# First self attention: the output projection by three products of split factors

## The chip, the core and the metric

One core of a Trainium2 chip runs the whole program. Its engines work side by side, each through its own queue in order, and meet at semaphores: TensorE (PE, matmuls, with its weight loads shown as PEld), VectorE (DVE), ScalarE (ACT), GpSimd (POOL) and SyncE (SP, which issues most DMAs). The metric is the device time of one execution in microseconds (us), the median of several runs.

## What is computed

Two transformer layers on x of shape 4 x 1024 x 256, f32. The change lies in the first step, the self attention of layer 0, followed by a residual and a layer norm:

```python
xq = jnp.einsum('bsh,oh->bso', x, wq)      # likewise xk, xv; 1024 outputs
xq = xq.reshape(bsz, N_HEADS, seqlen, HEAD_DIM)   # here 4 x 16 x 1024 x 64
scores = jnp.einsum('bhid,bhjd->bhij', xq, xk) * SCALE
scores = jax.nn.softmax(scores, axis=-1)
out = jnp.einsum('bhij,bhjd->bhid', scores, xv)
out = out.reshape(bsz, seqlen, N_HEADS * HEAD_DIM)
return jnp.einsum('bso,ho->bsh', out, wo)         # the output projection
...
x = _layernorm(x + _L0_attn_ref(x, ...), axis=-1)
```

The reshape makes a head of 64 token rows: 64 heads, each with 1024 x 1024 scores. The other steps (cross attention, a mixture of experts, a second self attention, a second cross attention, an MLP on chosen tokens) are not touched.

## The kernel before

`layer0_self_attention` works through 16 groups of 256 token rows, four heads each (j = 0 to 3); groups 1 to 13 are a hardware loop over `group`. Each engine walks the same Python code and emits only its own instructions, so the order of the code is the order of every queue, and `w.inc` / `w.at` keep the semaphore counts.

**A head** has four steps p = 0 to 3. In each, PE computes two of the eight 128-row blocks of transposed scores (`scores`, L726 to L732, into `psS`), ACT takes two exponentials of 128 x 1024 (`exponent`, L745, into the ring `pr`), POOL adds them to `total` (`add_up`, L760, seven adds per head), and PE multiplies the step before by V (`values`, L774, into `psO`). Meanwhile PE, DVE and ACT find the row maxima of the next head (`largest` L618/L619 and L626, `on_diagonal` L635, which I call `diag`), and after p = 3 `spread` (L645) brings them into `psX`, from where `seed_new` (L680 on DVE, L685 on ACT) and `keep_least` (L654, L658) set up `psS` for the next head.

**A head's end.** `take_out` (L784, ACT) copies `psO` to `oU`, without the softmax's division. The sum of the head's exponentials comes during the next head: at p = 1 PE sums `total` (`misc` "S", L441), DVE transposes and inverts (`turn_back`, L486, L793, L794, at p = 2), and POOL multiplies `oU` by the inverse (`divide`, L804, at p = 2, behind the adds of that step) into `oT`, two heads side by side. `take_out` of the next head waits for `ot`, so that `oU` is free:

```python
        def take_out(w):
...
                w.wait("pv", w.at("pv"))
                w.wait("ot", w.at("ot"))
                w.eng.activation(oU[:, :], psO[:, :], ACT.Copy).then_inc(sems["nm"], 1)
```

**Side tasks** (`misc`) fill PE between the steps; `TASKS` lists them by head and place. The Q and K projections of the next group (L427, six fp32r products of split factors) stand at p = 1, at p = 2 and twice at a head's end ("e"), where the first goes into `psM` and the second into `psO`: the second waits until `take_out` has read `psO`. The output projections ("O", L447, f32, eight products of 128 x 128 by 128 x 256 each, which the trace shows as sixteen matmuls) stand at p = 0 of heads 1 and 3. The residual, moments (`moments`), `root` (four small operations on POOL, L522 to L525, at p = 2) and `norm_out` (L534 on ACT, at p = 3) of the projected 128 rows follow in the same head; heads 0 and 2 have none of these.

**At the start**, `split` divides a weight matrix into a high part in fp32r (ACT) and the rest (DVE, L897 and L900), for wq, wk and wv. `wo` is used as it is.

Of the kernel before, what the change touches and what calls it, by code (L numbers as in the profile page):

```python
# [12 lines left out]
P = 128  # L13
D = 256
# [290 lines left out]
def layer0_self_attention(nc, x, wqT, wkT, wvT, woT, y):  # L305
# [13 lines left out]
    with ExitStack() as ctx:  # L319
        m = Room(nc, ctx, "a")  # L320
        wqh, wql, wkh, wkl, wvh, wvl = (m.sb(n, [P, 2, SEG * HD], F32R) for n in ("wqh", "wql", "wkh", "wkl", "wvh", "wvl"))
        wo = m.sb("wo", [P, KC, D])
# [31 lines left out]
        oT = m.sb("oT", [P, 2, KC, P])  # L354
# [14 lines left out]
                 "ad", "pv", "nm", "rec", "ot", "var", "pl", "rstd", "y", "yo", "dv")  # L369
# [36 lines left out]
        def misc(w, what, G, buf, k="M", more=True, out=True):  # L406
# [4 lines left out]
            if w.on("tensor"):  # L411
# [17 lines left out]
                elif kind == "V":  # L429
                    _, tt, c2 = what  # L430
                    if not out:
                        w.wait("wl", 3)
                    w.wait("xl", w.at("xl"))
                    for n, (xp, wp) in enumerate(((xh, wvh), (xh, wvl), (xl, wvh))):
                        for cc in range(2):
                            last = w.eng.matmul(ps[:, :], xp[:, cc, tt * P:(tt + 1) * P], wp[:, cc, c2 * 512:(c2 + 1) * 512],
                                                start=n == 0 and cc == 0, stop=n == 2 and cc == 1)
                elif kind == "S":
                    w.wait("ad", w.at("ad", 3 if more else 0))
                    for q in range(2):  # L440
                        last = w.eng.matmul(ps[q * HD:(q + 1) * HD, :], ones[:, 0:HD].bitcast(F32), total[:, buf, q * 512:(q + 1) * 512],  # L441
                                            start=True, stop=True)
                elif kind == "O":
                    w.wait("w", 16)
                    w.wait("ot", w.at("ot"))
                    for c in range(KC):
                        last = w.eng.matmul(ps[:, 0:D], oT[:, buf, c, :], wo[:, c, :], start=c == 0, stop=c == KC - 1)  # L447
# [29 lines left out]
            elif kind == "V":  # L477
                _, tt, c2 = what
                if w.on("scalar"):
                    w.wait("bv", w.at("bv"))  # L480
                    w.wait("mi", w.at("mi"))
                    w.eng.activation(vg[:, tt, c2 * 512:(c2 + 1) * 512], ps[:, :], ACT.Copy).then_inc(sems["ma"], 1)
# [316 lines left out]
        def divide(w, j):  # L799

            if w.on("gpsimd"):
                w.wait("nm", w.at("nm"))
                w.wait("rec", w.at("rec"))
                w.eng.tensor_tensor(oT[:, j // 2, :, (j % 2) * HD:(j % 2 + 1) * HD],  # L804
                                    oU[:, :].rearrange("p (c t) -> p c t", t=HD),
                                    rec[:, :].rearrange("p (c t) -> p c t", t=HD), ALU.mult).then_inc(sems["ot"], 1)
            w.inc("ot")

        def group(w, G, first=False, left=2):
# [17 lines left out]
            for j in range(GH):  # L827
# [11 lines left out]
                for p in range(KC // 2):  # L839
# [3 lines left out]
                    for i in (2 * p, 2 * p + 1):  # L843
                        exponent(w, i)
                        add_up(w, i, j % 2)
# [21 lines left out]
                    if p == 2 and not start:  # L867
                        turn_back(w)
                        divide(w, (j - 1) % GH)
# [20 lines left out]
        def walk(w):  # L890
            w.came = {}
            turns = ["S0", "S1", "S2", "S3", "0", "1", "M"]
            def split(n):
                hi, lo, full = ((wqh, wql, pr[:, 0:2, :]), (wkh, wkl, pr[:, 2:4, :]), (wvh, wvl, total[:, :, :]))[n]
                if w.on("scalar"):
                    w.wait(("wq", "wk", "wv")[n], 16)
                    w.eng.activation(hi[:, :, :], full, ACT.Copy).then_inc(sems["wh"], 1)  # L897
# [8 lines left out]
            for i in range(2 * KC):  # L906
                if i in (3, KC):
                    split((3, KC).index(i) + 1)
# [32 lines left out]
            divide(w, GH - 1)  # L941
# [26 lines left out]
        def _(eng):  # L968
            for t, src, n in ((pr[:, 0:2, :], wqT, "wq"), (pr[:, 2:4, :], wkT, "wk"), (total[:, :, :], wvT, "wv")):
                eng.dma_start(t, src.rearrange("(a p) o -> p a o", p=P)).then_inc(sems[n], 16)  # L970
            eng.dma_start(wo[:, :, :], woT.rearrange("(c p) e -> p c e", p=P)).then_inc(sems["w"], 16)
# [2032 lines left out]
```

## Time and profile before

| what | value |
|---|---|
| median of 3 runs | 2907.83 us (2907.33 to 2910.18) |
| profiled execution | 2896.75 us, its span 2895.0 us |
| PE busy | 2533.0 us, 87% |
| POOL, DVE, ACT busy | 56%, 63%, 54% |
| mean granted clock of PE | 0.937 of full speed |

The first self attention takes the first 1690 us of the span. A share of the span averages over stages with different limits; the stretch of a stage, and the timeline of one head in it, tell what ends a wait. A row of the timeline gives the start, the duration and, in brackets, how long the engine was idle before it and whose work ended that.

### The profile page before, as it was taken

Reading aid. Unit: us, or ns where it says so; the run is one execution under the profiler, and the core shown is the slowest. Engines: PE = TensorE matmul, PEld = TensorE weight load, DVE = VectorE, ACT = ScalarE, POOL = GpSimd, SP = SyncE. Lnnn points to the kernel's source line nnn. Section 1 sums busy time; section 2 is a strip of 40 time slices with the busy share of each in tenths; the row PEclk is TensorE's granted clock in tenths of the full one; section 3 lists DMA queues with packets and bytes.
Section 4 is the critical chain, followed back from the end, with each engine's and each line's share of the span. In section 5 each row is a group of like instructions: output and inputs, shape, how many; then the busy total and the mean of one; then the engine's idle time right before and its main releaser. Section 6 shows DMA issues by size and latency. Waiting matters only on the chain. (4 is left out here: it accounts for less than half of the span.)

```text
span 2895.0 us, 43888 instructions
## 1 busy us (share of the span) xinstructions
PE 2533.0 (87%) x12067; PEld 1413.7 (49%) x12067; DVE 1822.8 (63%) x3044; ACT 1576.4 (54%) x2568; POOL 1621.6 (56%) x1344
## 2 busy tenths in 40 slices
PE   6999999999999999999999959971994688698595
PEld 4554555555555555555554434540673344454264
DVE  4776777777777777777777635662334565468743
ACT  4666676766667676666766625640222343454334
POOL 2777677777767777776777733424334213333343
PEclk8999999999999999999999979985997699899798
DMA  7454444555445455545544220003992100000242
GB/s 185 121 132 117 124 129 123 136 126 130 121 123 129 122 136 127 130 121 124 129 122 107 57 93 2 2 20 124 382 341 92 32 0 1 31 2 10 57 127 88
DMA packets 413442, 309.49 MB, mean 107 GB/s; under 512 B 296951, under 2 KB 341407, under 8 KB 408351
## 3 DMA queue, kind: packets, MB, share of 16 engines
q1 hardware_dynamic: 397118, 238.27, 31.8%
q0 software_dynamic: 12272, 63.92, 6.3%
q10 hardware_dynamic: 3952, 6.08, 0.6%
q8 instruction: 50, 0.82, 0.1%
q14 instruction: 50, 0.40, 0.1%
HBM read 193.33 MB, written 94.13 MB: 99 GB/s over the span
## 5 line engine op out<-in xcount | busy, mean ns | idle before, releaser
L760 POOL TENSOR_TENSOR a_total<-a_total,a_pr 128x1024 f32<-128x1024 f32 x384 | 915.5, 2384 | 268.9 <-ACT a_pr L745 251.1
L626 DVE TENSOR_REDUCE a_nmax<-a_psX 128x1 f32<-128x1024 f32 x512 | 623.8, 1218 | 279.8 <-PE a_psX L619 279.8
L745 ACT ACTIVATE a_pr<-a_psS 128x1024 f32<-128x1024 f32 x512 | 496.5, 1022 | 364.1 <-PE a_psS L732 344.1
L774 PE MATMUL a_psO<-a_pr,a_vd 128*64 128x512 f32 x2048 | 492.5, 602 | 0.0
L726 PE MATMUL a_psS<-a_qA,a_kA 128*128 128x512 f32 x1024 | 292.1, 406 | 8.3 <-DVE a_psS L680 4.4
L618 PE MATMUL a_psX<-a_kA,a_qA 64*128 64x512 f32 x512 | 232.8, 455 | 35.5 <-DVE a_nmax L626 31.3
L760 POOL TENSOR_TENSOR a_total<-a_pr 128x1024 f32<-128x1024 f32 x64 | 152.1, 2377 | 192.5 <-ACT a_pr L745 192.5
L774 PEld LDWEIGHTS a_psO<-a_pr,a_vd 128*64 128x64 f32 x2048 | 129.9, 136 | 241.6 <-issue 240.5
L696 DVE COPY a_psS<-a_least 128x1024 f32<-128x1024 f32 x192 | 232.6, 1212 | 4.6 <-ACT a_pr L745 4.6
L635 ACT ACTIVATE a_diag<-a_ident,a_nmax 128x128 fp32r<-128x128 f32 x512 | 186.0, 401 | 88.1 <-DVE a_nmax L626 88.1
L619 PE MATMUL a_psX<-a_kB,a_qA 64*128 64x512 f32 x512 | 232.8, 455 | 0.0
L618 PEld LDWEIGHTS a_psX<-a_kA,a_qA 64*128 64x128 f32 x512 | 94.7, 185 | 238.1 <-DVE a_nmax L626 146.2
L726 PEld LDWEIGHTS a_psS<-a_qA,a_kA 128*128 128x128 f32 x1024 | 173.2, 190 | 58.4 <-issue 21.2
L705 ACT ACTIVATE a_psS<-a_least 128x1024 f32<-128x1024 f32 x192 | 197.0, 1026 | 0.3
L732 PE MATMUL a_psS<-a_qB,a_kB 64*128 64x512 f32 x512 | 187.6, 446 | 0.0
L730 PE MATMUL a_psS<-a_qB,a_kA 64*128 64x512 f32 x512 | 187.6, 446 | 0.0
L1204 DVE TENSOR_REDUCE c_nmx<-c_psM 128x4 f32<-128x308 f32 x256 | 109.6, 468 | 50.4 <-PE c_psM L1199 49.5
L680 DVE COPY a_psS<-a_psX 128x512 f32<-128x512 f32 x126 | 81.7, 694 | 82.9 <-PE a_psX L645 82.9
L447 PE MATMUL a_psM<-a_wo,a_oT 128*128 128x256 f32 x512 | 121.5, 391 | 3.3 <-POOL a_oT L804 3.3
L730 PEld LDWEIGHTS a_psS<-a_qB,a_kA 64*128 64x128 f32 x512 | 75.8, 185 | 93.6 <-issue 93.6
L2692 ACT ACTIVATE e_hT<-e_psH,e_wt 128x128 f32<-128x128 f32 x156 | 44.6, 368 | 127.9 <-PE e_psH L2684 127.9
L447 PEld LDWEIGHTS a_psM<-a_wo,a_oT 128*128 128x128 f32 x512 | 96.4, 193 | 27.0 <-issue 14.7
(423 smaller groups left out, 4881.1 us busy)
## 6 DMA issues: line engine op xcount, KB each, us to landing
a_qA<-a_qhi SPq DMA_DIRECT2D x248, 128.0 KB, 2.7
a_qB<-a_qlo SPq DMA_DIRECT2D x124, 256.0 KB, 3.8
a_vd<-a_vg SPq DMA_DIRECT2D x128, 128.0 KB, 2.3
a_kA<-a_khi SPq DMA_DIRECT2D x124, 128.0 KB, 2.6
a_kA<-a_klo SPq DMA_DIRECT2D x62, 256.0 KB, 3.6
a_qhi<-a_ph SPq DMA_DIRECT2D x120, 128.0 KB, 2.0
a_qlo<-a_pl SPq DMA_DIRECT2D x120, 128.0 KB, 2.1
a_khi<-a_ph SPq DMA_DIRECT2D x120, 128.0 KB, 2.0
```

What stands on the lines that cost most here:

```text
L447: last = w.eng.matmul(ps[:, 0:D], oT[:, buf, c, :], wo[:, c, :], start=c == 0, stop=c == KC - 1)
L618: w.eng.matmul(psX[:, 0, :], qA[0:HD, b, u * P:(u + 1) * P], kA[0:HD, b, 0:512], start=True, stop=True)
L619: w.eng.matmul(psX[:, 1, :], qA[HD:P, b, u * P:(u + 1) * P], kB[HD:P, b, :], start=True, stop=True)\
L626: w.eng.tensor_reduce(nmax[:, u:u + 1], psX[:, :, :].rearrange("p a k -> p (a k)"), AX.X, ALU.max, negate=True)\
L696: w.eng.tensor_copy(both(psS[:, 0, :, :]), least[:, :]).then_inc(sems["sv"], 1)
L705: w.eng.activation(both(psS[:, 1, :, :]), least[:, :], ACT.Copy).then_inc(sems["sa"], 1)
L726: w.eng.matmul(psS[:, n, q, :], kA[:, b, kc * P:(kc + 1) * P], qA[:, b, q * 512:(q + 1) * 512], start=False, stop=False, skip_group_check= ...
L730: low = w.eng.matmul(psS[:, 0, q, :], kA[0:HD, b, p * P:(p + 1) * P], qB[0:HD, b, cols], start=False, stop=True, skip_group_check=True)
L732: high = w.eng.matmul(psS[:, 1, q, :], kB[HD:P, b, p * P:(p + 1) * P], qB[HD:P, b, cols], start=False, stop=True, skip_group_check=True)
L745: w.eng.activation(pr[:, n, :], both(psS[:, i % 2, :, :]), ACT.Exp, scale=SCALE).then_inc(sems["e"], 1)
L760: w.eng.tensor_tensor(total[:, buf, :], first, pr[:, n, :], ALU.add).then_inc(sems["ad"], 1)
L774: last = w.eng.matmul(psO[q * HD:(q + 1) * HD, :], vd[:, b, kc, :], pr[:, n, q * 512:(q + 1) * 512], start=p == 0 and i == 0, stop=p == KC ...
```

## The change

Both factors of the output projection are split into a high part rounded to fp32r and the rest, and the projection becomes three fp32r products, high x high, high x low and low x high: 24 matmuls of 256 columns in place of eight f32 products. For that

- `divide` multiplies `oU` in place and signals `dq`, no longer `ot`;
- a new `split_out` copies `oU` to `oh` on ACT, after the eighth exponential of the head (i = 7), and subtracts on POOL, `oU - oh` into `ol`, between the adds of i = 6 and i = 7; this subtraction now signals `ot`, on which `take_out`, the projection, `turn_back` and the first add of a head wait as before;
- `woT` is loaded into `vg` at the start and split into `woh` and `wol` ahead of the thirteenth of sixteen Q and K pieces (i = 12), and the first write of `vg` by the V projections waits for that.

```diff
         wqh, wql, wkh, wkl, wvh, wvl = (m.sb(n, [P, 2, SEG * HD], F32R) for n in ("wqh", "wql", "wkh", "wkl", "wvh", "wvl"))
-        wo = m.sb("wo", [P, KC, D])
+        woh, wol = (m.sb(n, [P, KC, D], F32R) for n in ("woh", "wol"))
         ident = m.sb("ident", [P, P])
...
         inv = m.sb("inv", [P, 512 // 32])
-        oT = m.sb("oT", [P, 2, KC, P])
+        oh, ol = (m.sb(n, [P, 2, KC, P], F32R) for n in ("oh", "ol"))
         res = m.sb("res", [P, 2, D])
...
-                 "ad", "pv", "nm", "rec", "ot", "var", "pl", "rstd", "y", "yo", "dv")
+                 "ad", "pv", "nm", "rec", "dq", "oh", "ot", "var", "pl", "rstd", "y", "yo", "dv")
         sems = {n: m.sem(n) for n in names + tuple(f"so{n}" for n in range(PIECES))}
...
                 elif kind == "O":
-                    w.wait("w", 16)
+                    w.wait("wl", 4)
                     w.wait("ot", w.at("ot"))
-                    for c in range(KC):
-                        last = w.eng.matmul(ps[:, 0:D], oT[:, buf, c, :], wo[:, c, :], start=c == 0, stop=c == KC - 1)
+                    for n, (op, wp) in enumerate(((oh, woh), (oh, wol), (ol, woh))):
+                        for c in range(KC):
+                            last = w.eng.matmul(ps[:, 0:D], op[:, buf, c, :], wp[:, c, :],
+                                                start=n == 0 and c == 0, stop=n == 2 and c == KC - 1)
                 last.then_inc(sems["mi"], 1)
...
                     w.wait("bv", w.at("bv"))
+                    if not out:
+                        w.wait("wl", 4)
                     w.wait("mi", w.at("mi"))
...
-        def divide(w, j):
+        def divide(w):
             if w.on("gpsimd"):
                 w.wait("nm", w.at("nm"))
                 w.wait("rec", w.at("rec"))
-                w.eng.tensor_tensor(oT[:, j // 2, :, (j % 2) * HD:(j % 2 + 1) * HD],
-                                    oU[:, :].rearrange("p (c t) -> p c t", t=HD),
-                                    rec[:, :].rearrange("p (c t) -> p c t", t=HD), ALU.mult).then_inc(sems["ot"], 1)
+                w.eng.tensor_tensor(oU[:, :], oU[:, :], rec[:, :], ALU.mult).then_inc(sems["dq"], 1)
+            w.inc("dq")
+
+        def split_out(w, j):
+
+
+            def chunks(t):
+                return t[:, j // 2, :, (j % 2) * HD:(j % 2 + 1) * HD]
+
+            whole = oU[:, :].rearrange("p (c t) -> p c t", t=HD)
+            if w.on("scalar"):
+                w.wait("dq", w.at("dq"))
+                w.eng.activation(chunks(oh), whole, ACT.Copy).then_inc(sems["oh"], 1)
+            w.inc("oh")
+            if w.on("gpsimd"):
+                w.wait("dq", w.at("dq"))
+                w.wait("oh", w.at("oh"))
+                w.eng.tensor_tensor(chunks(ol), whole, chunks(oh).bitcast(F32), ALU.subtract).then_inc(sems["ot"], 1)
             w.inc("ot")
...
                         exponent(w, i)
+                        if i == KC - 1 and not start:
+                            split_out(w, (j - 1) % GH)
                         add_up(w, i, j % 2)
...
                         turn_back(w)
-                        divide(w, (j - 1) % GH)
+                        divide(w)
                     if p == 3 and outs:
...
             def split(n):
-                hi, lo, full = ((wqh, wql, pr[:, 0:2, :]), (wkh, wkl, pr[:, 2:4, :]), (wvh, wvl, total[:, :, :]))[n]
+                hi, lo, full = ((wqh, wql, pr[:, 0:2, :]), (wkh, wkl, pr[:, 2:4, :]), (wvh, wvl, total[:, :, :]),
+                                (woh, wol, vg[:, :, :].rearrange("p a (c e) -> p (a c) e", e=D)))[n]
                 if w.on("scalar"):
-                    w.wait(("wq", "wk", "wv")[n], 16)
+                    w.wait(("wq", "wk", "wv", "w")[n], 16)
                     w.eng.activation(hi[:, :, :], full, ACT.Copy).then_inc(sems["wh"], 1)
...
             for i in range(2 * KC):
-                if i in (3, KC):
-                    split((3, KC).index(i) + 1)
+                if i in (3, KC, KC + 4):
+                    split((3, KC, KC + 4).index(i) + 1)
                 misc(w, ("QK"[i // KC], i % KC), 0, 0, turns[i % 7], out=False)
...
             turn_back(w)
-            divide(w, GH - 1)
+            divide(w)
+            split_out(w, GH - 1)
             misc(w, ("O",), NG - 1, 1)
...
                 eng.dma_start(t, src.rearrange("(a p) o -> p a o", p=P)).then_inc(sems[n], 16)
-            eng.dma_start(wo[:, :, :], woT.rearrange("(c p) e -> p c e", p=P)).then_inc(sems["w"], 16)
+            eng.dma_start(vg[:, :, :].rearrange("p a (c e) -> p (a c) e", e=D), woT.rearrange("(c p) e -> p c e", p=P))\
+                .then_inc(sems["w"], 16)
             eng.preload_act_table(ACT.Exp)
             eng.wait_ge(sems["cst"], 5)
             walk(Writer(nc, eng, "scalar", sems))
```

POOL's order at the end of an odd head (head 3 of the first group, from p = 0): `a_total` is the running sum, `a_rstd` the four operations of `root`. Before:

```order
L760 TENSOR_TENSOR a_total<-a_total,a_pr 128x1024 x4
L522 TENSOR_TENSOR a_rstd<-a_mv,a_eps 128x1
L523 TENSOR_TENSOR a_rstd<-a_rstd,a_mhalf 128x1
L524 TENSOR_TENSOR a_rstd<-a_mv,a_rstd 128x1
L525 TENSOR_TENSOR a_rstd<-a_zero,a_rstd 128x1
L804 TENSOR_TENSOR a_oT<-a_oU,a_rec 128x8x64
L760 TENSOR_TENSOR a_total<-a_total,a_pr 128x1024 x2
```

After:

```order
L764 TENSOR_TENSOR a_total<-a_total,a_pr 128x1024 x4
L526 TENSOR_TENSOR a_rstd<-a_mv,a_eps 128x1
L527 TENSOR_TENSOR a_rstd<-a_rstd,a_mhalf 128x1
L528 TENSOR_TENSOR a_rstd<-a_mv,a_rstd 128x1
L529 TENSOR_TENSOR a_rstd<-a_zero,a_rstd 128x1
L808 TENSOR_TENSOR a_oU<-a_oU,a_rec 128x512
L764 TENSOR_TENSOR a_total<-a_total,a_pr 128x1024
L825 TENSOR_TENSOR a_ol<-a_oU,a_oh 128x8x64
L764 TENSOR_TENSOR a_total<-a_total,a_pr 128x1024
```

One 128 x 512 operation, the subtraction, has come between the last two adds, and the signal that frees `oU` has moved behind it.

ACT's order at the same head's end, from the step p = 3 on: `a_pr` are the last two exponentials, `a_diag` `on_diagonal`, `a_res` `norm_out`, `a_oU` `take_out`, the two `a_psS` `seed_new`, `a_least` `keep_least`. Before, behind the exponentials:

```order
L745 ACTIVATE a_pr<-a_psS 128x1024 x2
L635 ACTIVATE a_diag<-a_ident,a_nmax 128x128 x2
L534 ACTIVATE a_res<-a_res,a_rstd 128x256
L635 ACTIVATE a_diag<-a_ident,a_nmax 128x128
L784 ACTIVATE a_oU<-a_psO 128x512
L685 ACTIVATE a_psS<-a_psX 128x512 x2
L658 ACTIVATE a_least<-a_psX 128x512
```

After, with the exponentials:

```order
L749 ACTIVATE a_pr<-a_psS 128x1024 x2
L820 ACTIVATE a_oh<-a_oU 128x8x64
L639 ACTIVATE a_diag<-a_ident,a_nmax 128x128 x2
L538 ACTIVATE a_res<-a_res,a_rstd 128x256
L639 ACTIVATE a_diag<-a_ident,a_nmax 128x128
L788 ACTIVATE a_oU<-a_psO 128x512
L689 ACTIVATE a_psS<-a_psX 128x512 x2
L662 ACTIVATE a_least<-a_psX 128x512
```

The copy stands ahead of everything with which ACT ends the head.

## Rows read from the trace of the kernel before

**Rows 1.** The page, part 1: busy us, share of the span, instructions.

```profile
PE 2533.0 (87%) x12067; PEld 1413.7 (49%) x12067; DVE 1822.8 (63%) x3044; ACT 1576.4 (54%) x2568; POOL 1621.6 (56%) x1344
```

**Rows 2.** Windows: us, each engine's busy us, granted clock, DMA share, GB/s.

```profile
700.00:1000.00 300.00, 296.19 (x1483) 159.21 (x1483) 217.60 (x276) 205.61 (x345) 220.23 (x120) 1.00 0.50 127
```

**Rows 3.** Timeline, PE: start us, us, line, out<-in, count [idle, releaser].

```profile
787.96 0.51 PE L427 MATMUL a_psM<-a_xh,a_wkh 128*128 128x256 f32 x2
...
788.78 1.09 PE L726 MATMUL a_psS<-a_qA,a_kA 128*128 128x512 f32 x4
...
798.78 3.72 PE L447 MATMUL a_psM<-a_wo,a_oT 128*128 128x256 f32 x16
802.43 0.50 PE L618 MATMUL a_psX<-a_kA,a_qA 64*128 64x512 f32 x1
```

**Rows 4.** Timeline, POOL, an even head's end.

```profile
737.11 4.84 POOL L760 TENSOR_TENSOR a_total<-a_total,a_pr 128x1024 f32<-128x1024 f32 x2 [2.59 <-ACT a_pr L745]
741.91 1.28 POOL L804 TENSOR_TENSOR a_oT<-a_oU,a_rec 128x512 f32<-128x512 f32 x1
743.14 4.84 POOL L760 TENSOR_TENSOR a_total<-a_total,a_pr 128x1024 f32<-128x1024 f32 x2
```

**Rows 5.** Timeline, ACT, the same head's end.

```profile
741.05 1.94 ACT L745 ACTIVATE a_pr<-a_psS 128x1024 f32<-128x1024 f32 x2 [1.37 <-PE a_psS L732]
742.88 0.69 ACT L635 ACTIVATE a_diag<-a_ident,a_nmax 128x128 fp32r<-128x128 f32 x2
744.69 0.40 ACT L635 ACTIVATE a_diag<-a_ident,a_nmax 128x128 fp32r<-128x128 f32 x1 [1.12 <-DVE a_nmax L626]
745.31 0.60 ACT L784 ACTIVATE a_oU<-a_psO 128x512 f32<-128x512 f32 x1 [0.21 <-PE a_psO L774]
745.96 1.07 ACT L685 ACTIVATE a_psS<-a_psX 128x512 f32<-128x512 f32 x2
```

**Rows 6.** Timeline, PE, the same head's end.

```profile
745.19 0.73 PE L645 MATMUL a_psX<-a_diag,a_ones 128*128 128x512 f32 x2
...
746.47 0.40 PE L427 MATMUL a_psO<-a_xh,a_wqh 128*128 128x256 f32 x2
...
747.19 1.09 PE L726 MATMUL a_psS<-a_qA,a_kA 128*128 128x512 f32 x4
```

**Rows 7.** Timeline, POOL, an odd head's end.

```profile
716.82 1.27 POOL L804 TENSOR_TENSOR a_oT<-a_oU,a_rec 128x512 f32<-128x512 f32 x1
718.04 4.87 POOL L760 TENSOR_TENSOR a_total<-a_total,a_pr 128x1024 f32<-128x1024 f32 x2
```

**Rows 8.** Timeline, ACT, the same odd head's end.

```profile
716.96 0.59 ACT L534 ACTIVATE a_res<-a_res,a_rstd 128x256 f32<-128x256 f32 x1
718.27 0.40 ACT L635 ACTIVATE a_diag<-a_ident,a_nmax 128x128 fp32r<-128x128 f32 x1 [0.72 <-DVE a_nmax L626]
718.88 0.60 ACT L784 ACTIVATE a_oU<-a_psO 128x512 f32<-128x512 f32 x1 [0.21 <-PE a_psO L774]
```

**Rows 9.** Timeline, PE, the same odd head's end.

```profile
718.76 0.73 PE L645 MATMUL a_psX<-a_diag,a_ones 128*128 128x512 f32 x2
...
720.04 0.40 PE L427 MATMUL a_psO<-a_xh,a_wkh 128*128 128x256 f32 x2
```

**Rows 10.** Timeline, ACT, the last head.

```profile
1669.86 0.60 ACT L784 ACTIVATE a_oU<-a_psO 128x512 f32<-128x512 f32 x1 [0.68 <-POOL a_oT L804]
```

**Rows 11.** Timeline, DVE, at the start.

```profile
24.15 2.29 DVE L900 TENSOR_TENSOR a_wvl<-a_total,a_wvh 128x2048 fp32r<-128x2048 f32 x1 [0.49 <-ACT a_wvh L897]
```

**Rows 12.** Timeline, PE, and one window: two idles close together.

```profile
1581.73 0.49 PE L618 MATMUL a_psX<-a_kA,a_qA 64*128 64x512 f32 x1 [1.32 <-DVE a_nmax L626]
...
1582.86 2.07 PE L726 MATMUL a_psS<-a_qA,a_kA 128*128 128x512 f32 x4 [0.64 <-DVE a_psS L696]
...
1631.01 1.27 PE L726 MATMUL a_psS<-a_qA,a_kA 128*128 128x512 f32 x4 [0.63 <-DVE a_psS L696]
...
1583.00:1587.00 4.00, 4.00 (x14) 2.19 (x16) 1.55 (x2) 1.23 (x2) 1.58 (x1) 0.62 0.37 103
```

## The prediction

> **What bounds the kernel now.** I read the page first. TensorE (PE) is busy for 87% of the span, ahead of VectorE (DVE, 63%) and GpSimd (POOL, 56%) [rows 1]. The average hides that the changed stage is tighter: from 700 to 1000 us, in the middle of the first self attention, PE is busy for 296.19 of 300 us at a granted clock of 1.00, while ScalarE (ACT) has 205.61 and POOL 220.23 [rows 2]. PE sets the pace there, so a microsecond taken from PE is a microsecond of time, and a microsecond for which PE is made to wait is one too. There is 1% of slack to absorb it. ACT and POOL have a third and a quarter of their time free on average, but the change asks for them at one place, the end of each head, so I then read the timeline there engine by engine. There are two kinds of head end: 64 heads, of which those with j = 0 or 2 (even) have a plain end, and those with j = 1 or 3 (odd) carry the layer norm of a finished block too.
>
> **The output projection.** Before, one f32 projection is 8 products that the trace shows as 16 matmuls of 256 columns. It starts at 798.78 and the next matmul at 802.43: 3.65 us, 0.228 each [rows 3]. After, it is 24 fp32r products of 256 columns with other weights each time, the same form as the Q and K pieces. A piece of six behind `largest` takes from 787.96 to 788.78, 0.82 us [rows 3]; a piece in the middle of a stream 746.47 to 747.19, 0.72 us, 0.12 each [rows 6]. So 24 take 0.82 + 18 x 0.12 = 2.98 us, and a projection gets 0.67 us cheaper. There are 32 of them; 31 lie in the PE-bound stretch: **-20.8 us**. The matmuls rise by half in number and still cost less, since each takes half the time. The Trainium skill (TensorE: Matmul & The Clock Gate, Back-to-back issue gap) gives an isolated gap of columns / 2.4 GHz plus 2.5 ns, 109 ns for 256 columns; by that, a projection would be an estimated 2.6 us and the sum some 11 us lower. The row says 120 ns, so I keep the row.
>
> **What is added at a head's end.** The division now writes `oU` in place (same size, 1.28 us, no change). Behind the head's last exponential ACT copies `oU` to `oh` (128x512; the like copy L784 takes 0.60 us), and POOL subtracts `oU - oh` into `ol` (like L804, 1.28 us) between the last two adds. The word that decides is in a line that the diff doesn't touch: `take_out`, which copies the next head's `psO` over `oU`, waits for `ot`. Before, `ot` came with the division. Now it comes with the subtraction, because `oU` is still read by it. `take_out` stands in ACT's queue ahead of the two seed copies, the copy to `least` and the next head's exponentials, and PE waits for it before the second projection piece, which writes `psO`.
>
> **Even head's end, step by step.** POOL is busy without a break from 737.11: two adds, the division to 743.19, two adds to 747.98 [rows 4]. The sixth index's add ends at 743.14 + 2.38 = 745.52, so the subtraction can't start before 745.5, and ends at 745.47 + 1.28 = 746.75 (a start without a dependency comes 0.05 us before the end of the one ahead, as the division's does). ACT's own new copy is hidden: the exponentials end at 742.99 [rows 5], the division at 743.19, so the copy runs from 743.3 to 743.9 and two `diag` (0.69) to 744.6, before the third `diag` at 744.69, for which ACT waited 1.12 us. `take_out` started at 745.31, as soon as PE's last value product let it [rows 5]. It now waits for POOL to 746.75 + 0.10 = 746.85 (the 0.10 is the step from `diag`'s end, 745.09, to `spread` at 745.19 [rows 5, 6]), and ends at 747.45. PE's piece into `psO` began at 746.47 [rows 6]; now 747.55. With 0.11 for a first matmul after a wait, PE loses **1.19 us**. The seeds, 0.65 us behind `take_out`, are then just in time: the first ends at 748.1, when the scores begin at 748.4.
>
> **Odd head's end.** Four small layer-norm operations go ahead of the division, which therefore ends at 718.09, and the first add behind it at 718.04 + 2.39 = 720.43 [rows 7]. The subtraction: 720.38 to 721.66. ACT is hit earlier as well: its copy waits for the division, 718.19 to 718.79, and behind it queue two `diag`, the norm's 0.59 and the third `diag`, which ended at 718.67 and now ends near 720.4 [rows 8]. `spread` on PE slips from 718.76 to 720.5 [rows 9], a stall of 1.7 us that is a part of the whole, not more: `take_out` starts at 721.76, not 718.88 [rows 8], ends at 722.36, and the `psO` piece starts at 722.46, not 720.04 [rows 9]. With the 0.11: **2.53 us**.
>
> **Count.** The first split is issued in head 1, which has no norm yet. Short stalls: head 1 and the even heads 2 to 62, 32 x 1.19 = 38.1. Long stalls: odd heads 3 to 61, 30 x 2.53 = 75.9. In heads 58 to 62 there is no projection piece, but the next scores wait for ACT's seeds, behind the same `take_out`. Together **+114.0 us**. Nothing gives this back: each head's first exponential depends on the scores, and POOL, which then has its pause of 2.59 us before the fourth index [rows 4], is free in time. That a wait on this edge costs ACT real time is seen once before, in the last head, where `take_out` waited 0.68 us for L804 [rows 10].
>
> **Start and end.** The start gets a split of `woT` (a copy on ACT and, like the other weights' one, 2.29 us on DVE) ahead of the thirteenth of sixteen projection pieces. DVE works there without a pause, and the later pieces wait: **+2.3 us** [rows 11]; below, it could be nothing, above twice that, if ACT's copy counts as well. At the end the last add comes 1.28 later, copy and subtraction add 0.10 + 0.60 + 0.10 + 1.28 = 2.08 before the last projection, and that one saves about 1: **+2.4 us**.
>
> **Clock.** In this stage the clock stays at 1.00. The rows show what idling does: PE idled 1.32 us before 1581.73 and 0.64 before 1582.86; then four score matmuls took 2.07 us, and from 1583 to 1587 the granted clock was 0.62, a mix of 2.4 and 1.2 GHz: 0.38 x 4 = 1.5 us lost. Behind the like pair 48 us later, whose second idle is 0.63, the same matmuls took 1.27 us: nothing lost [rows 12]. An odd head's end now has two idles, 1.6 and 0.7 us, further apart than that pair; an even one has a single idle of 1.1, shorter than the first of that pair. I allow for a drop in one odd head of five: 30 x 0.2 x 1.5 = **+9 us**.
>
> **Sum.** -20.8 + 114.0 + 2.3 + 2.4 + 9 = +107 us. The profiled execution took 2896.75 us (span 2895.0) and would become 3004; the median of the runs, 2907.83, lies 11 us above it, so I forecast 3015 us, a ratio of 1.037.
>
> **Rivals.**
> (1) The clock drops in every odd head: 45 us in place of 9, 3051 us. For it: two idles with 2.3 us of waiting. Against: the pair above is denser and fell once and stayed once. The Trainium skill (TensorE: Matmul & The Clock Gate, Part 1) says that the gate goes by how busy PE was of late and knows two rates; by that this rival's chance hangs on how close together the two idles lie.
> (2) The other side: the copy and the subtraction are hidden as they look by the averages, because `take_out` doesn't come behind the subtraction. This decides at the point where the subtraction ends: before 745.3 in an even and 718.8 in an odd head it would cost nothing, and the rest would be -20.8 + 4.7 = -16 us, 2892 us. For it: POOL is idle for a quarter. Against: POOL has no gap between 737.11 and the head's end, and misses those points by 1.5 and 2.9 us, with every operation in that count taken from a row.
> (3) A part is absorbed: the stalls are there, but seeds, reductions and adds that were late catch up in them, so that half of the price stays: 2955 us. For it: 1.3% of PE's time in the stage is idle, waits that a shift could swallow [rows 2]. Against: that is 1.3 us per group of four heads, which come behind the scores and move along with them.
> (4) The fp32r projections cost what an f32 matmul costs, 0.228 each: 5.5 us in place of 3.65, 31 x 1.8 = 56 us in place of -20.8: 3092 us. Against: rows 6.
>
> **How the numbers follow.** Forecast 0.80; (1) 0.09; (2) 0.04; (3) 0.05; (4) 0.02. Unknown sizes: stalls of 1.08 and 2.42 without the first-matmul term (-7), a projection cheaper by 0.8 (-4), no clock loss (-9), start -2: about 2992. Upwards the clock in every odd head: 3051. Range 2990 to 3052. About 0.2% is what a measurement of this kernel can tell from no change; faster by more than that 0.04 (rival 2), within it 0.01, slower 0.95.
>
> **What would show it.** In the profile after: ACT's `take_out` group with idle time before it, ended by POOL's `ol`, about 1.8 us in 32 heads and, behind a later `diag`, 1.4 in 30, near 100 us in all; `oh` waits for POOL, little in even heads and over a microsecond in odd ones; a group of four heads takes 6 us more (2 x 1.19 + 2 x 2.53 - 2 x 0.67); PE's busy share from 700 to 1000 falls from 99% to about 92%; a projection takes 3.0 us. The forecast is wrong if `take_out` doesn't wait, or if PE's waits before `psO` are well below 1 us.

## The result, and the profile after

| | before | after |
|---|---|---|
| median, six runs each, side by side | 2906.68 us (2902.31 to 2910.18) | 3005.76 us (3003.2 to 3009.68) |
| profiled execution | 2896.75 us | 3004.84 us |

The kernel became slower by a ratio of 1.0343 (95% interval 1.033 to 1.0357): 99 us between the medians, 108 between the two profiled executions. The forecast was 3015 us, +107.

The page's first part and the window of [rows 2], after:

```profile
PE 2544.6 (85%) x12323; PEld 1425.4 (47%) x12323; DVE 1827.9 (61%) x3045; ACT 1609.6 (54%) x2633; POOL 1698.0 (57%) x1408
...
700.00:1000.00 300.00, 278.85 (x1430) 150.63 (x1429) 203.82 (x255) 199.33 (x337) 219.50 (x124) 0.99 0.47 119
```

PE's busy time from 700 to 1000 us fell from 296.19 to 278.85 us, from 99% to 93%. No other engine took its place as the bound: ACT and POOL are both at or below where they were in [rows 2]. PE waits. For whom, the view of the waits says (0 to 1800 us; engine, tile and line that waits, whose work ended the wait, us in total, how often, the longest):

```profile
ACT a_oU L788 <- POOL a_ol L825: 107.1, 63, 2.5
...
ACT a_oh L820 <- POOL a_oU L808: 69.5, 64, 7.0
...
PE a_psO L427 <- ACT a_oU L788: 47.1, 57, 0.9
PE a_psX L649 <- ACT a_diag L639: 40.1, 30, 1.4
```

The chain can be read off: the subtraction (L825, POOL) holds up `take_out` (L788, ACT) in 63 heads, `take_out` holds up the piece into `psO` (PE) 57 times by 0.83 us on the mean, and in 30 odd heads a late third `diag` (L639) holds up `spread` (L649) by 1.34 us.

**An even head's end**, the timeline (start, us, line, out<-in, count, idle before and who ended it) of POOL, ACT and PE, answering [rows 4 to 6]:

```profile
779.59 2.38 POOL L764 TENSOR_TENSOR a_total<-a_total,a_pr 128x1024 f32<-128x1024 f32 x1
781.92 1.28 POOL L808 TENSOR_TENSOR a_oU<-a_oU,a_rec 128x512 f32<-128x512 f32 x1
783.15 2.38 POOL L764 TENSOR_TENSOR a_total<-a_total,a_pr 128x1024 f32<-128x1024 f32 x1
785.46 1.31 POOL L825 TENSOR_TENSOR a_ol<-a_oU,a_oh 128x512 fp32r<-128x512 f32 x1
786.70 2.41 POOL L764 TENSOR_TENSOR a_total<-a_total,a_pr 128x1024 f32<-128x1024 f32 x1
...
783.24 0.63 ACT L820 ACTIVATE a_oh<-a_oU 128x512 fp32r<-128x512 f32 x1 [0.33 <-POOL a_oU L808]
783.77 0.68 ACT L639 ACTIVATE a_diag<-a_ident,a_nmax 128x128 fp32r<-128x128 f32 x2
784.69 0.40 ACT L639 ACTIVATE a_diag<-a_ident,a_nmax 128x128 fp32r<-128x128 f32 x1 [0.24 <-DVE a_nmax L630]
786.87 0.60 ACT L788 ACTIVATE a_oU<-a_psO 128x512 f32<-128x512 f32 x1 [1.77 <-POOL a_ol L825]
...
787.52 0.51 PE L427 MATMUL a_psO<-a_xh,a_wqh 128*128 128x256 f32 x2 [0.89 <-ACT a_oU L788]
```

POOL has no gap in this stretch, with the subtraction behind the first of the two adds. ACT's new copy is done at 783.87, long before it is needed: not the copy, but POOL's queue sets the subtraction's start. The subtraction ends at 786.77 and `take_out` starts 0.10 later. The third `diag` is on time, and PE loses its time once, ahead of `psO`.

**An odd head's end**, the same views, answering [rows 7 to 9]:

```profile
752.95 1.27 POOL L808 TENSOR_TENSOR a_oU<-a_oU,a_rec 128x512 f32<-128x512 f32 x1
754.18 2.35 POOL L764 TENSOR_TENSOR a_total<-a_total,a_pr 128x1024 f32<-128x1024 f32 x1
756.49 1.29 POOL L825 TENSOR_TENSOR a_ol<-a_oU,a_oh 128x512 fp32r<-128x512 f32 x1
...
754.25 0.63 ACT L820 ACTIVATE a_oh<-a_oU 128x512 fp32r<-128x512 f32 x1 [1.67 <-POOL a_oU L808]
...
755.87 0.39 ACT L639 ACTIVATE a_diag<-a_ident,a_nmax 128x128 fp32r<-128x128 f32 x1
757.87 0.60 ACT L788 ACTIVATE a_oU<-a_psO 128x512 f32<-128x512 f32 x1 [1.62 <-POOL a_ol L825]
...
756.30 0.72 PE L649 MATMUL a_psX<-a_diag,a_ones 128*128 128x512 f32 x2 [1.36 <-ACT a_diag L639]
...
758.52 0.80 PE L427 MATMUL a_psO<-a_xh,a_wkh 128*128 128x256 f32 x2 [0.79 <-ACT a_oU L788]
```

Here the division comes later, so the copy waits for it, and the `diag` behind it in ACT's queue has no idle time before it any more (0.72 in [rows 8]): it runs as soon as the queue lets it. PE idles twice, 1.36 and 0.79 us. In this head the clock fell as well: the piece took 0.80 where [rows 9] have 0.40, and from 758 to 762 the granted clock was 0.57.

**The projection**, PE's timeline, answering [rows 3]:

```profile
790.26 1.21 PE L448 MATMUL a_psM<-a_woh,a_oh 128*128 128x256 f32 x8
791.31 1.10 PE L448 MATMUL a_psM<-a_wol,a_oh 128*128 128x256 f32 x8
792.24 1.10 PE L448 MATMUL a_psM<-a_woh,a_ol 128*128 128x256 f32 x8
793.27 0.50 PE L622 MATMUL a_psX<-a_kA,a_qA 64*128 64x512 f32 x1
```

24 products from 790.26 to 793.27, 3.01 us, against 3.65.

**Where the 108 us are.** I measured each head as the time from the end of its predecessor's last exponential to the end of its own, in both traces. What follows an even head got longer by 0.50 us behind head 0 of a group and by 0.43 behind head 2 (medians of the heads without a drop of the clock), which is a stall of about 1.1 less the 0.6 or so that a projection gained; what follows an odd head got longer by 2.41 to 2.44, and by 3.7 to 3.9 where the clock fell. Head 1, the first with a stall, has no norm yet; what follows it got longer by 1.05. Up to the last head's last exponential that comes to 1.05 + 31 x 0.465 + 30 x 2.43 + 1.5 at the start = 89.9 us. The measured shift there is 101.9 us, and the 12 left over go with the clock: ten stretches at half clock (1.2 of 2.4 GHz) up to that point (at 168, 543, 758, 1188, 1403 and 1618 us, and behind heads 58 to 61, where no projection pieces are left), against one before. Behind the last head the stage's end costs another 1.9. The last 4 us lie in the later stages, whose code is the same and whose length differs by more than that between the profiled executions of this case (1206 to 1218 us).

### The profile page after: what moved, and what is told of

Read it like the earlier page. It is cut to its first block and busy times, and to the rows that moved or that the text cites. A ratio compares the mean times of both kernels' runs of the same rounds, so it can differ in the third digit from the quotient of the medians.

```text
span 3003.0 us, 44611 instructions
## 1 busy us (share of the span) xinstructions
PE 2544.6 (85%) x12323; PEld 1425.4 (47%) x12323; DVE 1827.9 (61%) x3045; ACT 1609.6 (54%) x2633; POOL 1698.0 (57%) x1408
## 5 line engine op out<-in xcount | busy, mean ns | idle before, releaser
L730 PE MATMUL a_psS<-a_qA,a_kA 128*128 128x512 f32 x1024 | 299.0, 413 | 10.9 <-DVE a_psS L684 4.4
L639 ACT ACTIVATE a_diag<-a_ident,a_nmax 128x128 fp32r<-128x128 f32 x512 | 184.7, 396 | 33.5 <-DVE a_nmax L630 33.5
L475 DVE TENSOR_TENSOR a_pl<-a_psM,a_ph 128x256 fp32r<-128x256 f32 x177 | 73.9, 417 | 80.2 <-ACT a_ph L471 78.4
L1212 POOL CAST c_qR<-c_qF 128x512 fp32r<-128x512 f32 x64 | 40.4, 633 | 114.9 <-ACT c_qF L1207 114.8
```

Of the source, the lines that this page charges most:

```text
L639: w.eng.activation(diag[:, u * P:(u + 1) * P], ident[:, :], ACT.Copy, scale=nmax[:, u:u + 1]).then_inc(sems["dg"], 1)
L730: w.eng.matmul(psS[:, n, q, :], kA[:, b, kc * P:(kc + 1) * P], qA[:, b, q * 512:(q + 1) * 512], start=False, stop=False, skip_group_check= ...
```

## The experiments

The forecast was near, so the question is whether it was near for its reasons. The theory: `take_out` comes one to one behind the subtraction; in odd heads the wait of ACT's copy for the division is nested inside that; the fp32r product itself is a gain; the clock adds some. The rivals: the two waits of an odd head add up; the product isn't cheaper; something else than the release of `oU` sets the price. "`take_out` at +3.96" means 3.96 us after the end of the head's last exponential. It stood at +2.4 to +2.5 before in nearly all heads, and stands at +3.96 in even heads and +5.27 in odd ones after (medians).

### The product back to f32

```diff
                 elif kind == "O":
...
-                    for n, (op, wp) in enumerate(((oh, woh), (oh, wol), (ol, woh))):
-                        for c in range(KC):
-                            last = w.eng.matmul(ps[:, 0:D], op[:, buf, c, :], wp[:, c, :],
-                                                start=n == 0 and c == 0, stop=n == 2 and c == KC - 1)
+                    for c in range(KC):
+                        last = w.eng.matmul(ps[:, 0:D], oh[:, buf, c, :], woh[:, c, :], start=c == 0, stop=c == KC - 1)
```

`oh` and `woh` become f32 copies. The subtraction, the copies and the split of the weights stay in place, but the low factors aren't used.

> Changed kernel with the projection back to one f32 product (the copy goes into an f32 tile, the subtraction and the split of the weights are still done, their results not used for the product). Everything else and all orders as in the changed kernel. Theory: a projection takes 3.65 us again in place of 2.98, so 31 x 0.67 = 21 us more than the changed kernel, 3026 us. If the fp32r products gained nothing: 3006. If they gained as by 109 ns a matmul: 3037.

Measured: 3030.26 us (3027.9 to 3040.83), ratio 1.044 (1.0422 to 1.0457). A projection, PE's timeline:

```profile
798.22 3.72 PE L449 MATMUL a_psM<-a_woh,a_oh 128*128 128x256 f32 x16
801.87 0.50 PE L622 MATMUL a_psX<-a_kA,a_qA 64*128 64x512 f32 x1
```

3.65 us again, and the heads with a projection are 0.64 us longer than in the changed kernel (median): 32 x 0.64 = 20 of the 25 us between the two medians. The profiled execution was the slowest of this kernel's, 10 us above its median. In it the heads together are 28 us longer than in the changed kernel, the 20 and the clock, whose half-clock time is worth 18 single stretches against 13. The stalls are the same. So the arithmetic is a gain of 0.64 us each time, and the loss lies in the split's waits and in what they cost of the clock. Rival (4) falls.

### The subtraction one add earlier

```diff
-                    for i in (2 * p, 2 * p + 1):
-                        exponent(w, i)
-                        if i == KC - 1 and not start:
-                            split_out(w, (j - 1) % GH)
-                        add_up(w, i, j % 2)
+                    if p == 3 and not start:
+                        exponent(w, 6)
+                        exponent(w, 7, early=1)
+                        split_out(w, (j - 1) % GH)
+                        add_up(w, 6, j % 2, 1)
+                        add_up(w, 7, j % 2)
...
```

Both last adds now come behind the subtraction in POOL's queue; `early` and the added argument only keep the counts of the semaphores right.

> Changed kernel with GpSimd's subtraction ahead of the add of i=6 instead of behind it; ScalarE's copy stays behind the last exponential. Theory (take_out waits for the subtraction): from the trace after, z being the end of a head's last exponential, the copy ends at z+1.0 in an even and z+2.3 in an odd head, the subtraction at z+2.4 and z+3.7, so take_out starts at z+2.5 in even heads (before the change 2.3 to 2.5, after it 3.95) and at z+4.0 in odd ones (5.27), there held by ScalarE's own queue, no longer by GpSimd. Stalls: 32 x 0.1 and 30 x 1.8 = 57 us in place of about 111, so about 2946 us. Rival A (the extra 1.9 us of work on two engines costs this, wherever it stands in the queues): as after, 3006 us. Rival B (only GpSimd's place in the queue matters, ScalarE's copy is hidden everywhere): 2890 us.

Measured: 2934.09 us (2925.8 to 2934.25), ratio 1.0101 (1.0083 to 1.012), some 70 us less than the changed kernel. Even heads lose nothing any more (`take_out` at +2.47); odd heads have it at +3.79 and lose 1.35 to 1.43 each. POOL at the end of an odd head, and the waits from 100 to 1690 us:

```profile
777.55 1.28 POOL L808 TENSOR_TENSOR a_oU<-a_oU,a_rec 128x512 f32<-128x512 f32 x1
779.63 1.27 POOL L825 TENSOR_TENSOR a_ol<-a_oU,a_oh 128x512 fp32r<-128x512 f32 x1 [0.81 <-ACT a_oh L820]
780.85 4.87 POOL L764 TENSOR_TENSOR a_total<-a_total,a_pr 128x1024 f32<-128x1024 f32 x2
...
ACT a_oU L788 <- POOL a_ol L825: 7.3, 26, 0.3
...
PE a_psX L649 <- ACT a_diag L639: 40.2, 30, 1.4
```

The wait for the subtraction fell from 107 us (0 to 1800 us; 99.6 in this window) to 7, although every instruction is still there. One add's place in a queue was worth some 70% of the loss. The wait for `diag` stayed, and the odd heads lose 1.4 us with it. I had expected 1.8 per odd head, and `take_out` at +4.0, held by ACT's own queue; it came at +3.79, and POOL still held it in 26 heads, by 0.3 us at most.

### Two buffers for `oU`

```diff
-        oU = m.sb("oU", [P, 512])
+        oU = m.sb("oU", [P, 2, 512])
...
-        def take_out(w):
+        def take_out(w, b, back):
...
-                w.wait("ot", w.at("ot"))
-                w.eng.activation(oU[:, :], psO[:, :], ACT.Copy).then_inc(sems["nm"], 1)
+                w.wait("ot", w.at("ot", back))
+                w.eng.activation(oU[:, b, :], psO[:, :], ACT.Copy).then_inc(sems["nm"], 1)
...
-                take_out(w)
+                take_out(w, b, 1)
```

`take_out` writes the other buffer and waits for the subtraction of the head before (`back` = 1). For room, the inverse sums are written over `turned`, with a wait for that. The order on all engines is that of the changed kernel.

> Changed kernel with two buffers oU in turn, so that take_out doesn't wait for the subtraction of the head before but for that of two heads before; rec is written over turned to make room; orders of all queues unchanged. Theory: take_out no longer waits for GpSimd in any head; even heads lose nothing, odd heads still lose 1.75 to 1.85 us, since ScalarE's copy waits for the division with the third diag, and so spread, queued behind it. 30 x 1.8 = 54 us of stalls, about 2944 us, the same as with the subtraction moved. Rival A (the extra work itself): 3006. Rival B (only take_out's wait counts): 2890.

Measured: 2935.71 us (2933.47 to 2936.12), ratio 1.0114 (1.0097 to 1.0131). The waits from 100 to 1690 us:

```profile
ACT a_oU L788 <- PE a_psO L778: 7.7, 32, 0.3
...
PE a_psX L649 <- ACT a_diag L639: 40.1, 30, 1.4
```

`take_out` never waits for POOL, with the subtraction where the changed kernel has it. Even heads lose 0, odd ones 1.4 (expected: 1.8): the same as in the last experiment, by the other way. So the price of an even head is the release of `oU` and nothing else, and an odd head has a second price of 1.4 behind it.

### ACT's copy behind the third `diag`

```diff
                 values(w, KC // 2 - 1, b)
                 if more:
                     on_diagonal(w, KC - 1)
+                if not start:
+                    split_out(w, (j - 1) % GH, "copy")
                 take_out(w)
```

One buffer again, and the subtraction at the changed kernel's place. Only the copy moves, to where nothing waits behind it but `take_out`.

> Changed kernel with one buffer and GpSimd's order as it is; only ScalarE's copy is moved from behind the last exponential to behind the third diag, so spread is no longer late in odd heads. Theory (in odd heads the two delays lie inside one another: take_out waits for the subtraction in any case): odd heads gain nothing, take_out stays at z+5.3 and the scores' delay at 2.45 us; PE idles once for 2.4 us instead of 1.3 and 0.8. Even heads lose 0.25 us more, since the copy now ends at z+2.7 and the subtraction starts 0.25 later. 3006 + 32 x 0.25 = 3014 us, plus 1.4 us for each clock drop that the longer single idle brings (up to 40). Rival (the two delays add up, 1.4 for spread and 1.1 for take_out): 3006 - 30 x 1.4 = 2964 us.

Measured: 3033.31 us (3027.92 to 3034.37), ratio 1.0446 (1.0429 to 1.0463), slower than the changed kernel (ratio 1.0343). An odd head's end on POOL and ACT, and PE behind it:

```profile
760.95 1.27 POOL L808 TENSOR_TENSOR a_oU<-a_oU,a_rec 128x512 f32<-128x512 f32 x1
762.18 2.39 POOL L764 TENSOR_TENSOR a_total<-a_total,a_pr 128x1024 f32<-128x1024 f32 x1
764.51 1.27 POOL L828 TENSOR_TENSOR a_ol<-a_oU,a_oh 128x512 fp32r<-128x512 f32 x1
...
762.40 0.40 ACT L639 ACTIVATE a_diag<-a_ident,a_nmax 128x128 fp32r<-128x128 f32 x1 [0.72 <-DVE a_nmax L630]
762.71 0.62 ACT L821 ACTIVATE a_oh<-a_oU 128x512 fp32r<-128x512 f32 x1
765.88 0.60 ACT L788 ACTIVATE a_oU<-a_psO 128x512 f32<-128x512 f32 x1 [2.55 <-POOL a_ol L828]
...
766.52 0.50 PE L427 MATMUL a_psO<-a_xh,a_wkh 128*128 128x256 f32 x2 [2.19 <-ACT a_oU L788]
```

The third `diag` is on time again, 0.72 idle before it as in [rows 8]. It gave nothing: `take_out` of odd heads still stands at +5.26 (median), and PE has its waits as one idle of 2.19 in place of 1.36 and 0.79. The two waits of an odd head are nested, as the prediction had it ("a part of the whole, not more"), and the rival in which they add up (2964 us) falls. In even heads the copy came a little too late now (+4.22, 32 x 0.26 = 8 us). The clock took most of the rest: up to the last head, half-clock time worth 24 single stretches against 13 in the changed kernel (two of whose ten are longer), which at 1.4 us each is 15 us. 8 + 15 = 23, and the heads together got longer by 24.5.

### Two buffers, the whole split at the head's very end

```diff
                         exponent(w, i)
-                        if i == KC - 1 and not start:
-                            split_out(w, (j - 1) % GH)
                         add_up(w, i, j % 2)
...
+                if not start:
+                    split_out(w, (j - 1) % GH)
```

This is on top of the two buffers, and the count for which `take_out` waits moves along. The added lines stand behind the Q and K pieces of the head's end. The edit is meant to free ACT's queue ahead of the third `diag`.

> As with two buffers, and copy and subtraction stand at the very end of a head's code, behind the projection pieces' copies and all seven adds, where ScalarE idles before the next head's first exponential (about 1 us) and GpSimd idles before its first add (1.7 to 3 us). Theory: no stall is left in any head; what stays is the projection's gain of 0.67 us x 31, 1.5 us at the start and about 2 at the end: 2889 to 2893 us, faster than the kernel before by 0.5%. Rival A (the extra work itself costs): near 3006. Rival C (the copy now delays the next head's first exponential by up to 0.6 us in every head): 2893 + 38 = 2930.

Measured: 2918.38 us (2915.24 to 2920.06), ratio 1.0056 (1.0039 to 1.0072). A miss: 2889 to 2893 was expected. PE at the projection, POOL's subtraction ahead of it, and the waits from 0 to 1800 us:

```profile
751.21 1.27 POOL L825 TENSOR_TENSOR a_ol<-a_oU,a_oh 128x512 fp32r<-128x512 f32 x1 [0.74 <-ACT a_oh L820]
...
752.63 1.20 PE L447 MATMUL a_psM<-a_woh,a_oh 128*128 128x256 f32 x8 [0.68 <-POOL a_ol L825]
...
PE a_psM L447 <- POOL a_ol L825: 31.0, 32, 5.4
```

All waits at the head's end are gone, and a new one took their place: the projection, at p = 0 of the next head, needs the subtraction that was just put off. The heads with a projection gain some 0.6 and lose 1.0. The others lose nothing, so the late copy itself costs nothing.

### Two buffers, the split placed by its reader

A projection reads the outputs of two heads, and stands at p = 0 of heads 1 and 3. The split issued in head 0 or 2 is the later one of its two and is read at once. The split issued in head 1 or 3 is read a whole head later. So it stays at p = 3 in heads 0 and 2, which have no layer norm that delays the division, and goes to the very end in heads 1 and 3. This is on top of the two buffers:

```diff
-                        if i == KC - 1 and not start:
+                        if i == KC - 1 and b == 0 and not start:
                             split_out(w, (j - 1) % GH)
...
-                take_out(w, b, 1)
+                take_out(w, b, 1 - b)
...
+                if b == 1:
+                    split_out(w, j - 1)
```

> Two buffers oU, and the place of the split by head: in heads 0 and 2 copy and subtraction stay at p = 3 (the two-buffer run lost nothing there), in heads 1 and 3 they stand at the head's very end (the late-split run lost nothing by that copy; its loss was the projection of the next head waiting for a subtraction that had just been queued, 31 us in 32 waits, and the split that is late here is needed only a head and a half later). Theory: no stall in any head and no wait of the projection: the first stage ends 17 to 19 us earlier than in the kernel before (31 x 0.67 = 20.8 gained, 1 to 2 lost at the start, 1 to 2 at the end), 2884 us, ratio 0.994. Rival (extra work on ScalarE and GpSimd costs something of its own, in every head 0.1 to 0.3 us): 2890 to 2903.

Measured: 2883.95 us (2880.15 to 2889.61), ratio 0.9954 (0.9942 to 0.9967): 0.5% faster than the kernel before, little but clear of the noise, and 4% faster than the changed one. The window of [rows 2] and the waits from 0 to 1700 us:

```profile
700.00:1000.00 300.00, 296.10 (x1550) 161.69 (x1548) 220.84 (x280) 215.32 (x360) 236.00 (x133) 1.00 0.50 129
...
ACT a_oU L788 <- PE a_psO L778: 14.2, 63, 0.3
...
PE a_psM L447 <- POOL a_ol L825: 5.4, 1, 5.4
```

PE is as busy as before, and `take_out` is released by PE, as before. The only wait for the subtraction is the last projection's. Each head with a projection is some 0.6 us shorter than before (medians 0.63 behind head 0 of a group, 0.58 behind head 2), the others are unchanged within 0.1, and the last head's last exponential ends 19.0 us earlier: the term of -20.8 us, with about 1 us at the start against it. Of these 19 us, 15 arrive in the medians.

### The subtraction done twice

```diff
                 w.wait("oh", w.at("oh"))
+                w.eng.tensor_tensor(chunks(ol), whole, chunks(oh).bitcast(F32), ALU.subtract).then_inc(sems["dr"], 1)
+                w.wait("dr", w.at("dr", -1))
                 w.eng.tensor_tensor(chunks(ol), whole, chunks(oh).bitcast(F32), ALU.subtract).then_inc(sems["ot"], 1)
```

The changed kernel with one subtraction more; the second one signals.

> Changed kernel with the subtraction done twice, the second behind the first on GpSimd, and only the second signals ot. Theory (the stall is the distance from PE's last value product to the subtraction's end, one to one): each of 62 heads loses 1.29 + 0.08 us more, and the end 1.4: 3006 + 86 = 3092 us; more clock drops may add up to 20. If ScalarE's copy behind the division were what holds the odd heads, they would lose nothing more: 3006 + 32 x 1.37 = 3050. If the stall came from elsewhere: 3006.

Measured: 3155.78 us (3149.28 to 3158.26), ratio 1.088 (1.0864 to 1.0896). The waits from 100 to 1690 us, the window of [rows 2], and PE in an odd head (twice) and in an even one:

```profile
ACT a_oU L788 <- POOL a_ol L827: 163.8, 54, 3.1
...
PE a_psO L427 <- ACT a_oU L788: 117.2, 54, 2.3
...
700.00:1000.00 300.00, 266.50 (x1313) 146.15 (x1311) 187.20 (x238) 182.27 (x307) 212.79 (x123) 0.94 0.42 108
...
757.37 0.74 PE L649 MATMUL a_psX<-a_diag,a_ones 128*128 128x512 f32 x2 [1.33 <-ACT a_diag L639]
...
760.93 0.50 PE L427 MATMUL a_psO<-a_xh,a_wqh 128*128 128x256 f32 x2 [2.11 <-ACT a_oU L788]
...
789.28 0.80 PE L427 MATMUL a_psO<-a_xh,a_wkh 128*128 128x256 f32 x2 [2.23 <-ACT a_oU L788]
```

`take_out` moved from +3.96 to +5.29 and from +5.27 to +6.59, 1.33 us in each kind of head for 1.3 us of added subtraction: one to one, with nothing absorbed. For 62 heads that is 82 us. The measured heads grew by 153.5 us together. The other 71 go with the clock: half-clock time worth 66 single stretches against 13, so 53 more at 1.3 each. My expectation allowed the clock up to 20 us, and that size was wrong by more than a factor of three.

## Why the prediction was right, point by point

- **PE bounds the stage, so its stalls are time.** Right. A head lost about what PE idled, and a little more: 1.1 us for 0.89 of idle in an even head, 2.4 for 1.36 + 0.79 in an odd one. A piece takes 0.10 us more behind a wait, which is part of the difference. The added subtraction went through one to one.
- **The projection, -20.8 us.** Forecast 2.98 us, measured 3.01; a gain of about 0.6 per head, shown by its undoing (0.64) and again in the version that beats both kernels (0.63 and 0.58). By the isolated gap of the Trainium skill (TensorE: Matmul & The Clock Gate, Back-to-back issue gap), 109 ns for 256 columns, a projection would have been an estimated 2.6 us. The stream in the trace is slower than that: 3.01 us / 24 = 125 ns.
- **Even heads, 1.19 us.** Measured 1.13 in head 0 of a group and 1.0 in head 2, against the version placed by reader, which has no stall. Each step of the reckoning shows in the rows: the subtraction behind one add, the 0.10 us to ACT, `take_out`'s 0.60, PE's 0.89 us of idle.
- **Odd heads, 2.53 us.** Measured 2.4 to 2.5. That `spread`'s stall is a part of the whole was the step that could have gone the other way; the experiment with the copy moved settles it. The size of that part, 1.7 us, was too high: measured 1.36. From the division's end to `spread` the prediction had 2.4 us, the trace has 2.08, since each ACT operation starts some 0.09 us before the end of the one ahead (755.87 against 755.95, for one). The sum wasn't touched by it, as the part lies inside the whole. It is why the 1.8 us expected for the subtraction earlier and for the two buffers came out as 1.4.
- **Start +2.3, end +2.4.** Measured 1.5 or less (the first head's end varies by a microsecond between runs) and 1.9. At the end, the last projection waited 5.4 us for POOL where it had waited 3.3.
- **Clock, +9 us.** Measured about 12, but not spread as I had it. In the steady groups 5 of some 28 odd heads had a drop, one in five to six, each about 1.4 us; the rest of the cost came behind heads 57 to 61, in the last two groups, where even heads had drops too.
- **Rivals.** (2), hidden: falls, it would need POOL to have a gap. (3), half absorbed: falls, by the doubled subtraction. (4): falls. (1), the clock in every odd head: it was not so here, but it is how this kernel behaves with a little more waiting, as the doubled subtraction shows.
- **Signs.** 107 us of `take_out` idle against "near 100"; a group of four heads 5.8 us longer (0.50 + 2.41 + 0.43 + 2.44) against 6; PE at 93% against 92%.
- **What the sum was made against.** The profiled execution before lay some 10 us under the median of its runs, the one after only 1. So the profiles differ by 108 and the medians by 99, and the forecast from the median came out 9 us high.
- **Luck.** That the sum, 107, and the two profiles, 108, agree to a microsecond is in part luck. The stalls, the start and the end were put some 6 us too high, the clock 3 too low, and 4 us come from later stages that the change doesn't touch and the sum didn't have.

## What to carry to other kernels

Where a step gets a second reader of a buffer, find out who waits for that buffer to come free, and where the last reader stands in its queue: a quarter of idle time on that engine doesn't help if its queue is full at that moment. A split (or any helper step) is placed by when its result is read: the same split cost 99 us at one place, and gained 15 us with two buffers and places chosen per head. When two waits appear at one point, ask whether they are nested before adding them, and before removing the earlier one alone.

## What the runs showed that I had not expected

**How often the clock drops goes with how long and how close together the idles are.** In the steady part of the stage (100 to 1600 us), PE's idles at a head's end and the half-clock stretches were, in one profiled execution of each kernel:

| kernel | idles in an odd head, even head | half-clock stretches |
|---|---|---|
| before, and the version placed by reader | none; none | 1 (at 1582, at 1563) |
| subtraction earlier, two buffers | 1.36; none | 0 |
| changed kernel | 1.36 and 0.79; 0.89 | 5 |
| f32 product | 1.36 and 0.79; 0.89 | 9 |
| copy behind `diag` | 2.19 in one; about 1.15 | 16 |
| subtraction twice | 1.33 and 2.11; 2.23 | 44, some of them double |

All of them also have an idle of up to 1.3 us once in a group, elsewhere. The drops of the changed kernel, the f32 product and the copy behind `diag` all lie behind odd heads. In this part one idle of 1.36 us never cost any clock; a single one of 2.19 did in more than half of the odd heads. Right behind this part the same late `diag` did cost clock, with a second idle close to it. At the end of head 59 no projection piece follows `spread`, and in the version with two buffers PE's timeline has

```profile
1599.28 0.74 PE L649 MATMUL a_psX<-a_diag,a_ones 128*128 128x512 f32 x2 [1.20 <-ACT a_diag L639]
1600.90 1.82 PE L730 MATMUL a_psS<-a_qA,a_kA 128*128 128x512 f32 x4 [0.88 <-DVE a_psS L684]
```

with half clock from 1601.2 us; the version with the subtraction earlier has the like two idles and half clock from 1602.0.

The changed kernel and the f32 product have the same idles, but five drops and nine: behind the first drop the distances are 375 us once and then 215 (two groups) or twice that in the one kernel, and, but for the first, 109 and 218 in turn in the other, where a group is 1.3 us longer. That the group's length makes the difference is only my reading, and no run changed that length alone. The f32 product's profiled execution was also the slowest of its four, at a mean granted clock of 0.928 against 0.930 and 0.931, so the count may differ by some drops between executions of one kernel. Each stretch cost 1.3 to 1.5 us. The Trainium skill (TensorE: Matmul & The Clock Gate, Part 1) has a gate that goes by how busy PE was of late, and on a time of its own, not the kernel's. The repeating distances would fit that; no run here shows it.

**Joining two waits can cost more than either.** With the copy behind the third `diag`, the two short idles of an odd head became a single one of the same sum, and the half-clock time nearly doubled. Of the 28 us that this edit cost against the changed kernel, 8 are the later copy in even heads, and some 15 are the clock.
